# A three-part decoder layer on one core: value matmuls of four heads together over the column groups, and self-attention scores over all four quarters of the array

## What is computed

```
x = layernorm(x + attn(x))        # 16 heads of 16, causal, rotary, softmax over 64 keys
x = layernorm(x + xattn(x, ctx))  # each 64x256 sequence is read as 256 positions of 64 features:
                                  # 8 heads of 8, band |i-j| <= 64, softmax, then relu, times ctx, w_ct
x = layernorm(x + ffn(x))         # ternary weights, silu(gate)*up, rms norm, 256 -> 1024 -> 256
```

## Time and profile before

| | |
|---|---|
| median of 3 runs | 1548.48 us (1545.73 to 1553.0) |
| profiled execution | 1549.6 us from first to last instruction |
| PE busy | 1386.2 us, 89% |
| DVE / POOL / ACT busy | 1063.8 / 944.6 / 688.0 us |
| mean granted clock of PE | 0.936 of 2.4 GHz |
| share of PE in the chain that ended last | 78% |

### The profile page before, as it was taken

The page is one execution under the profiler, slowest core; times in us unless marked ns, Lnnn a source line. Parts: engine busy times, 40 slices in busy tenths (PEclk is TensorE's granted clock), DMA queues, the critical chain, the costliest instruction groups (busy, mean ns, idle before and its releaser), DMA issues.

```text
span 1549.6 us, 31054 instructions
## 1 busy us (share of the span) xinstructions
PE 1386.2 (89%) x10392; PEld 800.2 (52%) x10456; DVE 1063.8 (69%) x2215; ACT 688.0 (44%) x1331; POOL 944.6 (61%) x1867
## 2 busy tenths in 40 slices
PE   2367899999999999999999999999999999999985
PEld 1144455555555555555555555555555555555442
DVE  2677677777777667677777767767777777776532
ACT  1221345545445444545444444544544544454542
POOL 2443576776676666676666666667666666663531
PEclk8665899999999999999999999999999999999996
DMA  5000000000000000000000000000000000000000
GB/s 156 14 9 3 15 12 8 16 16 15 16 15 14 9 15 12 17 16 15 15 18 15 5 17 15 12 17 16 15 15 18 13 7 15 12 9 8 8 8 7
DMA packets 26950, 25.65 MB, mean 17 GB/s; under 512 B 6161, under 2 KB 26001, under 8 KB 26769
## 3 DMA queue, kind: packets, MB, share of 16 engines
q1 hardware_dynamic: 26768, 23.37, 5.3%
HBM read 14.18 MB, written 4.19 MB: 12 GB/s over the span
## 4 chain that ended last, share of the span: by engine, by line
PE 78%; ACT 8%; DVE 7%; issue 5%; POOL 1%; SPq 1%; DMA 0%; ACTq 0%; POOLq 0%; DVEq 0%
PE ps L397 13%; PE ps L399 9%; PE ps L510 8%; PE ps L569 7%; PE ps L370 5%; PE ps L484 5%; PE ps L422 4%; PE ps L454 4%; PE ps L590 4%; ACT hsplit L756 2%; PE ps L469 2%; PE ps L372 2%; PE ps L435 2%; ACT hT L759 2%; ACT prob L683 2%
## 5 line engine op out<-in xcount | busy, mean ns | idle before, releaser
L683 ACT ACTIVATE prob<-ps 128x384 f32<-128x384 f32 x512 | 248.0, 491 | 428.8 <-PE ps L372 428.7
L983 DVE TENSOR_REDUCE rowmax<-ps 128x2 f32<-128x384 f32 x512 | 279.6, 550 | 70.0 <-PE ps L385 55.1
L841 POOL TENSOR_TENSOR hsum<-hsum,minus_half 128x8 f32<-128x8 f32 x128 | 211.4, 1661 | 97.3 <-DVE hsum L1024 97.3
L397 PE MATMUL ps<-prob,v_pad 128*32 128x192 f32 x1024 | 267.5, 344 | 1.5 <-ACT headsT L689 1.5
L399 PE MATMUL ps<-prob,v_pad 128*32 128x192 f32 x1024 | 255.5, 332 | 0.0
L793 POOL TENSOR_SCALAR_AFFINE_SELECT prob<-prob 128x128 f32<-128x128 f32 (+1 forms) x512 | 185.8, 363 | 102.0 <-ACT prob L683 101.9
L804 POOL TENSOR_SCALAR base<-mv 128x1 f32<-128x1 f32 x96 | 32.5, 339 | 257.0 <-DVE mv L917 257.0
L796 POOL TENSOR_SCALAR_AFFINE_SELECT prob<-prob 128x256 f32<-128x256 f32 (+1 forms) x512 | 182.7, 357 | 0.0
L1072 DVE TENSOR_SCALAR high<-ps,bx_col 128x512 f16<-128x512 f32 x128 | 103.6, 809 | 85.2 <-PE ps L510 81.7
L510 PE MATMUL ps<-x,wx_qk 128*128 128x256 f32 x512 | 141.0, 400 | 5.5 <-DVE q_rows L1075 5.3
L399 PEld LDWEIGHTS ps<-prob,v_pad 128*32 128x32 f32 x1024 | 114.7, 112 | 56.7
(11 more groups left out here) (147 smaller groups left out, 2891.4 us busy)
## 6 DMA issues: line engine op xcount, KB each, us to landing
v_swap<-v_own SPq DMA_DIRECT2D x64, 68.0 KB, 2.0
xin<-in_x SPq DMA_DIRECT2D x32, 128.0 KB, 2.2
enc<-in_ctx SPq DMA_DIRECT2D x32, 128.0 KB, 2.2
out<-yout SPq DMA_DIRECT2D x32, 128.0 KB, 1.7
prob<-in_w_gu SPq DMA_DIRECT2D x4, 512.0 KB, 7.2
prob<-in_w_proj SPq DMA_DIRECT2D x2, 512.0 KB, 8.7
q_rows<-negmax SPq DMA_DIRECT2D x64, 8.0 KB
wqkv<-in_Wkv SPq DMA_DIRECT2D x1, 512.0 KB, 3.9
```

The source lines that it names most:

```text
L397: mm(out[:, 0:QW], v_pad[:, tile.buf, 0, u, :], prob[:, u, 0, :], start=True, stop=False, skip_group_check=True, tile_position=(0, 32 * hq))
L683: copy(prob[:, u, :, :].rearrange("p a b -> p (a b)"), ps[:, STB + u % 2, 0:2 * QW], ACT.Exp, scale=float(XD) ** -0.5).then_inc(S["exp"], 1)
L841: ins = g.tensor_tensor(hsum[:, 1, h], hsum[:, 0, h], minus_half[:, h], ALU.pow)
L983: v.tensor_reduce(rowmax[:, tile.buf, 8 * hq + 2 * ng:8 * hq + 2 * ng + 2], ps[:, MXB + u % 2, 0:2 * QW].rearrange("p (a b) -> p a b", a=2 ...
```

## The change

`values` takes a group of four units `4*ng` to `4*ng+3` in one go, when the last of them would have been due (slots 14, 2, 6 and 10), and waits once for their `c_sel`. Within it the order is all four units' first key blocks, then all four second ones; the four differ in `hq`, and so in the column group of the array. `e_scores` writes both masks first, then goes over `f`, `r` and `b`, so that neighbouring matmuls are in four different 64x64 quarters. The amount of arithmetic is the same.

```
-            def values(tile, u):
-                g, hq = u // 4 % 2, u % 4
-                if u % 2 == 0:
-                    pe.wait_ge(S["sel"], tile.at(UNITS // 2, u // 2 + 1))
-                if u == 0 and not tile.first:
+            def values(tile, ng):
+                g = ng % 2
+                pe.wait_ge(S["sel"], tile.at(UNITS // 2, 2 * ng + 2))
+                if ng == 0 and not tile.first:
                     pe.wait_ge(S["ot"], tile.at(2, 0))
-                if u == 8:
+                if ng == 2:
                     pe.wait_ge(S["ot"], tile.at(2, 1))
-                out = ps[32 * hq:32 * hq + 32, OTB, g * 256:(g + 1) * 256]
-                mm(out[:, 0:QW], v_pad[:, tile.buf, 0, u, :], prob[:, u, 0, :], start=True, stop=False, ...)
-                last = mm(out[:, 64:256], v_pad[:, tile.buf, 1, u, :], prob[:, u, 1, :], start=False, stop=True, ...)
+                cols = (slice(0, QW), slice(64, 256))
+                for kb in range(2):
+                    for hq in range(4):
+                        out = ps[32 * hq:32 * hq + 32, OTB, g * 256:(g + 1) * 256]
+                        last = mm(out[:, cols[kb]], v_pad[:, tile.buf, kb, 4 * ng + hq, :], prob[:, 4 * ng + hq, kb, :], ...)
...
-                def e_scores(r):
+                def e_scores():
...
+                    mm(ps[:, G6, :], identb[:, :], causal[:, :], start=True, stop=False, skip_group_check=True)
+                    bank_read((A, "qk", 2, 1), (M, "rows", 4, 3))
+                    mm(ps[:, G7, :], identb[:, :], causal[:, :], start=True, stop=False, skip_group_check=True)
                     for f in range(2):
-                        for b in range(2):
+                        for r in range(2):
+                            for b in range(2):
...
-                    if tile:
-                        values(tile, u)
+                    if tile and u % 4 == 3:
+                        values(tile, u // 4)
```

More of the change, by code:

```diff
@@ L386, in max_scores @@
                    start=True, stop=True).then_inc(S["mx"], 1)
-            def values(tile, u):
-                g, hq = u // 4 % 2, u % 4
-                if u % 2 == 0:
-                    pe.wait_ge(S["sel"], tile.at(UNITS // 2, u // 2 + 1))
-                if u == 0 and not tile.first:
+            def values(tile, ng):
+                g = ng % 2
+                pe.wait_ge(S["sel"], tile.at(UNITS // 2, 2 * ng + 2))
+                if ng == 0 and not tile.first:
                     pe.wait_ge(S["ot"], tile.at(2, 0))
-                if u == 8:
+                if ng == 2:
                     pe.wait_ge(S["ot"], tile.at(2, 1))
-                out = ps[32 * hq:32 * hq + 32, OTB, g * 256:(g + 1) * 256]
[L397 to L401, removed]
+                cols = (slice(0, QW), slice(64, 256))
+                for kb in range(2):
+                    for hq in range(4):
+                        out = ps[32 * hq:32 * hq + 32, OTB, g * 256:(g + 1) * 256]
+                        last = mm(out[:, cols[kb]], v_pad[:, tile.buf, kb, 4 * ng + hq, :], prob[:, 4 * ng + hq, kb, :],
+                                  start=kb == 0, stop=kb == 1, skip_group_check=True, tile_position=(0, 32 * hq))
+                if g == 1:
                     last.then_inc(S["ot_ps"], 1)
@@ L443, in e_transpose @@
                     last.then_inc(S["qkT_ps"], 1)
-                def e_scores(r):
[L446 to L451, removed]
-                    for f in range(2):
-                        for b in range(2):
[L454 to L460, removed]
+                def e_scores():
+                    pe.wait_ge(S["qkT"], E.at(1, 1))
+                    bank_read((A, "xnT", 1, 1), (C, "x2_c", 2, 1))
+                    mm(ps[:, G6, :], identb[:, :], causal[:, :], start=True, stop=False, skip_group_check=True)
+                    bank_read((A, "qk", 2, 1), (M, "rows", 4, 3))
+                    mm(ps[:, G7, :], identb[:, :], causal[:, :], start=True, stop=False, skip_group_check=True)
+                    for f in range(2):
+                        for r in range(2):
+                            for b in range(2):
+                                last = mm(
+                                    ps[64 * b:64 * b + 64, G6 + r, 256 * f:256 * f + 256]
+                                    .rearrange("p (e k) -> p e k", e=4),
+                                    qT[64 * r:64 * r + 64, f, 64 * b:64 * b + 64],
+                                    kT[64 * r:64 * r + 64, f, :, 64 * b:64 * b + 64],
+                                    start=False, stop=True, skip_group_check=True, tile_position=(64 * r, 64 * b))
+                            if f == 1:
+                                last.then_inc(S["s_ps"], 1)
                 def e_transpose_probs(c):
@@ L617, in step @@
                     if k == 3 and E:
-                        e_scores(0)
-                        e_scores(1)
+                        e_scores()
                     if k == 4 and P:
```

## The result

The changed kernel takes 1503.55 us (median of 4 runs, 1500.92 to 1509.43), before 1550.74 (4 runs, 1545.73 to 1558.11): ratio 0.9703, 95% interval 0.9674 to 0.9733. That is 47 us less, where 61 were forecast (1487). The profiled execution spans 1500.0 us instead of 1549.6.

A forecast was written before the change was run, and what follows sets the result against it. PE's matmul starts were taken to bound the kernel; 13.2 + 26.1 = 39.3 us a step, plus 1.6 for the clock, 40.9 against 43.1: 2.2 saved in 28 steps, 62 us, giving 1487 us (1455 to 1520; with rivals 1438 to 1550).

The forecast's parts named there:

- What bounds before: Whole step: PE's matmuls from start to start set its 42.3 us, so savings count fully until another engine is late.
- Four streams at once: Value matmuls: four column groups run together, 0.80 us a group instead of 3.08 for four units, 9.1 us a step less.
- the staircase: Value groups: program order binds passes, so four column groups overlap only two deep, 1.5 us a group; chance 0.10.
- The scores: `e_scores`: two masks in a row and one round of scores for both halves, 1.55 us instead of 2.66.
- PE's work is not what counts: Whole step: PE alone would need 31.1 us, less than DVE's 33.1, so waits decide and the gain can't be 10.
- A step at the full clock: Whole step without falls of the clock: 13.2 us for slots 7 to 12 plus 26.1 for the others, 39.3.
- Slots 7 to 12: A chain through DVE, POOL and ACT keeps this stretch at 13.2 us, so 3.1 us saved there don't count.
- The other slots: Slots outside 7 to 12: 29.1 us falls to 21.7 of work, plus 4.4 of new waits, 26.1.
- The clock: Falls in slots 3 to 6 and 7 to 12 cost 1.6 us a step (bounds 0 and 4.5), before 0.8.
- The first (clock as before): Rival: the clock falls no more often than before, 3.6 to 4.2 us a step saved, about 1440 us; chance 0.13.
- the second: Rival: program order binds the passes in value groups and `e_scores`, step 44.1 us, 1577 in all; chance 0.10.
- The third, low clock for much of the step: Rival: thinner PE work lowers the clock, deciding from 2.5 paid falls a step; at 3.3, 1580 us; chance 0.12.

The follow-up runs named there:

- the run with fillers in slots 5 and 12: Changed kernel plus filler matmuls whose output goes unread, 16 in slot 5 and 20 in slot 12: 1466.04 us, ratio 0.9456 to the kernel before.
- the order test: Changed kernel with each group's eight value matmuls ordered by unit instead of key blocks first: 1509.47 us, ratio 0.971 to the kernel before.
- pairs: Changed kernel with value units taken two at a time every second slot instead of in fours: 1482.61 us, ratio 0.9546 to the kernel before.
- pairs with fillers: The kernel with value units in pairs, plus 8 filler matmuls in slot 5 and 16 in slot 12: 1503.51 us, ratio 0.9697 to the kernel before.

## Why the prediction was right, and where it was off

- **What bounds before.** Right. `e_scores` alone saves its full price a step.
- **Four streams at once.** Right, to 0.01 us: 0.79 for 0.80. Neither the 0.97 us that I estimated from the 2.38x for three column groups in the Trainium skill (TensorE: Matmul & The Clock Gate, Part 3: Packing small matmuls) came, nor the staircase (1.5 us).
- **The scores.** Right: 1.56 for 1.55.
- **PE's work is not what counts.** Right in kind: the chain's share of PE fell from 78% to 45%, and PE was busy 88% of the time from 200 to 1300 us (forecast 85), DVE 75% (77).
- **A step at the full clock, forecast 39.3.** Right: 39.0 to 39.2. No step of the changed kernel is free of the low clock, but each part of one is, somewhere. The step that begins at 686 us has it behind L584 only:

```profile
686.18 0.33 PE L519 MATMUL ps<-ident,rowmax 128*128 128x128 f32 x1
692.34 0.25 PE L370 MATMUL ps<-q_rows,k_rows 26*128 26x192 f16 x1
...
695.58 0.24 DVE L1025 TENSOR_SCALAR hsum<-hsum,rot 128x32 f32<-128x32 f32 x1 [0.16 <-DVE hsum L1023]
702.10 0.55 POOL L870 TENSOR_TENSOR hss<-hss,expo 128x1 f32<-128x1 f32 x1
702.68 1.15 ACT L757 ACTIVATE hsplit<-hid,hss 128x1024 f16<-128x1024 f32 x1 [0.69 <-POOL hss L870]
705.31 0.61 PE L584 MATMUL ps<-ident,hsplit 128*128 128x128 f16 x8 [2.33 <-DVE heads L1098]
...
817.47 0.25 PE L370 MATMUL ps<-q_rows,k_rows 26*128 26x192 f16 x1
829.37 0.61 PE L584 MATMUL ps<-ident,hsplit 128*128 128x128 f16 x8 [0.80 <-DVE heads L1098]
849.15 0.33 PE L519 MATMUL ps<-ident,rowmax 128*128 128x128 f32 x1
```

  From L519 to slot 7 it is 6.2 us and from there to L584 13.0; from 829.37 to 849.15, in a step with no low clock there, 19.8 (20.0 in others). That is 39.0 to 39.2, and the whole steps of the run with fillers in slots 5 and 12 are as long.
- **Slots 7 to 12.** Right, and for the reasons given: 13.0 for 13.2. L1025 starts 3.24 us after slot 7 where L1024 did 2.36 after it, so DVE had fallen behind by 0.9; L757 starts as soon as POOL's power ends, where L756 stood a microsecond behind ACT's exponential. The two nearly cancel. In the step at 817.47 the stretch is 11.9 only since slot 7 itself is late there: the clock was low in slot 6, and the other engines' chain went on.
- **The other slots, forecast 26.1.** Right: 26.0 to 26.2. Of the 4.4 us of waits, most came nearly as priced: from start to start in that step, 1.4 us for 1.5 before L552, 0.5 for 0.6 and 1.0 for 1.1 for `rowmax`, 0.7 for 0.7 and 0.3 for 0.5 for the rows. In ten steps `gated` is waited for in slot 0 ahead of the rows.
- **The clock, forecast 1.6.** Nearly right: some 1.8 us a step, what a mean step of 41.3 us has over 39.1 and the 0.4 at the loop's turns (below). The mean of 0.89 was forecast (0.89 to 0.94), falls in slots 3 to 6 and 7 to 12 too, and that much of it is hidden: at 0.89 over 41.3 us PE is at the lower level for some 9 us and would lose 4.5. What is lost in slots 3 to 6 comes back in part in slots 7 to 12 (11.9 for 13.0), and a low clock in slots 10 and 11 there costs nothing before a wait. A third place was not foreseen, slot 14, two slots behind the wait for the heads:

```profile
708.00:711.40 3.40, 3.40 (x14) 2.41 (x12) 1.27 (x3) 2.10 (x4) 3.04 (x9) 0.51 0.01 2
```

  It makes 21.2 us of the 19.8 from L584 to L519. Before, the clock cost 0.7 us a step (forecast 0.8).
- **What was left out.** The wait before L370 at the loop's turns, `issue` in the table above: 7.6 us before and 10.3 after, 0.3 and 0.4 us a step.
- **Sum.** The first and last L517 and L519 of 25 steps:

```profile
275.87 0.33 PE L517 MATMUL ps<-ident,rowmax 128*128 128x128 f32 x1
1357.72 0.33 PE L517 MATMUL ps<-ident,rowmax 128*128 128x128 f32 x1
...
271.69 0.33 PE L519 MATMUL ps<-ident,rowmax 128*128 128x128 f32 x1
1303.25 0.33 PE L519 MATMUL ps<-ident,rowmax 128*128 128x128 f32 x1
...
L519 PE MATMUL ps<-ident,rowmax x32: 327/328/474, 158.3 to 1415.8; 128*128 128x128 f32 x32
```

  That is 43.3 us a step before and 41.3 after, where the forecast had 43.1 and 40.9: 2.0 saved for 2.2. And I had counted 28 such steps, but outside these 25 nothing is gained: the three distances ahead of them are 5.4 us shorter (with the earlier trace rows), the three behind 4.9 longer. Of the 12 us by which the forecast saving was too large some 6 are this count, some 5 the 0.2 us a step.
- **Rivals.** The first (clock as before) fell at once, the second by the group's 0.79 and the order test. The third, low clock for much of the step, came part of its way: 1.8 us of the 3.8 from which it would have decided.

## What to carry to other kernels

Small matmuls that leave column or row groups free can be packed (here four units in the time of one), and whether such matmuls start at once can be read from pairs that are already there; but price a bound engine's saving only until the next engine's chain is late, and look for what the removed work was covering: here the larger packing added next to nothing to the smaller one. When packing thins TensorE's program, read the granted clock of each stretch: matmuls that waited-for results leave room for can cost nothing and give back more than they take, and packing only as far as the waits allow (pairs, not fours) may be the better version without them.

## What was not expected of the hardware

- Two streams cost as much as four: a pair 0.78 us, a group of four 0.79, and sixteen passes in one column group 2.72.
- 36 matmuls a step that compute nothing made the kernel 2.5% faster (1466.04 against 1503.55), with the granted clock at 0.96 instead of 0.89. Eight more in slot 9 left it at 0.96, and the kernel was 11 us slower, though its steps at the full clock were no longer.
- At each turn of the loop PE stands idle with nothing shown that it waits for: 7.6 us in six turns before, 10.3 after, and 24.7 in pairs with fillers.
